# Attention on one core: the new keys' value product in three fp32r passes over split parts, and each reciprocal of a row sum taken one step later

## The reference, cut to what matters

```python
kc = k_cache[block_table].reshape(bsz, L, HK, D)
vc = v_cache[block_table].reshape(bsz, L, HK, D)
k_all = jnp.concatenate([kc, k], axis=1)
v_all = jnp.concatenate([vc, v], axis=1)
...
scores = jnp.einsum('bqhd,bkhd->bhqk', q, k_all) * SCALE
scores = jnp.where(valid[:, None, None, :], scores, -1e+30)
probs = jax.nn.softmax(scores, axis=-1)
o = jnp.einsum('bhqk,bkhd->bqhd', probs, v_all)
```

## Time and profile before

| | |
|---|---|
| median of three runs | 1268.01 us (1266.29 to 1268.69) |
| profiled execution, its own time | 1267.51 us |
| its span, first to last instruction | 1265.5 us |
| busy over the span: PE, PEld, DVE, ACT, POOL | 1232.9, 1036.5, 804.2, 789.2, 749.0 us |
| mean granted TensorE clock | 0.995 |
| attention of the first half, of the second | about 165 to 480 us, 800 to 1112 us |

### The profile page before, as it was taken

How to read it: one execution, slowest core, us unless ns; L and a number is a source line. 1 busy time by engine, 2 the same in 40 slices (tenths; PEclk the granted TensorE clock), 3 DMA queues, 4 the chain that set the end, 5 groups by cost and what they waited for, 6 DMA issues and landing times.

```text
span 1265.5 us, 28738 instructions
## 1 busy us (share of the span) xinstructions
PE 1232.9 (97%) x7378; PEld 1036.5 (82%) x7378; DVE 804.2 (64%) x1725; ACT 789.2 (62%) x2258; POOL 749.0 (59%) x884
## 2 busy tenths in 40 slices
PE   7899999999999999999998999999999999999998
PEld 6678889999999987866776888898999999888756
DVE  5976667667766776952329766676676677655422
ACT  5676677777777774432336666777787777744320
POOL 4344468888888874433233444588888888754330
PEclk9999999999999999999999999999999999999999
DMA  6343289999999955306144342889989999534300
GB/s 236 117 134 124 96 231 231 225 234 232 236 237 235 232 146 183 143 1 200 50 145 125 118 136 101 226 225 233 232 231 238 234 233 237 133 111 152 90 31 34
DMA packets 147979, 214.82 MB, mean 170 GB/s; under 512 B 24950, under 2 KB 119480, under 8 KB 142137
## 3 DMA queue, kind: packets, MB, share of 16 engines
q1 hardware_dynamic: 130568, 204.86, 59.7%
q10 hardware_dynamic: 17328, 9.04, 2.5%
HBM read 203.33 MB, written 10.49 MB: 169 GB/s over the span
## 4 chain that ended last, share of the span: by engine, by line
PE 84%; SPq 5%; DVE 3%; issue 3%; ACT 3%; DMA 1%; ACTq 1%; DVEq 0%
PE PS L1130 16%; PE PS L1098 8%; PE PS L1197 5%; PE PS L992 5%; PE PS L990 5%; PE PS L996 5%; PE PS L1188 5%; PE PS L1194 5%; PE PS L1140 4%; PE PS L976 2%; PE PS L1239 2%; PE PS L1063 2%; SPq L464 2%; PE PS L1065 2%; PE PS L1081 2%
## 5 line engine op out<-in xcount | busy, mean ns | idle before, releaser
L624 POOL TENSOR_TENSOR kv_parts<-kv,k_hi 128x544 fp32r<-128x544 f32 x192 | 258.0, 1344 | 55.0 <-ACT k_hi L806 54.9
L1130 PE MATMUL PS<-probT,kv 128*128 128x128 f32 x2048 | 271.9, 276 | 0.0
L584 POOL TENSOR_TENSOR ring_parts<-ring,kv_parts 128x512 fp32r<-128x512 f32 x96 | 126.2, 1320 | 217.4 <-ACT kv_parts L687 189.2
L1130 PEld LDWEIGHTS PS<-probT,kv 128*128 128x128 f32 x2048 | 250.5, 193 | 0.0
L847 ACT ACTIVATE ring<-ring,smin 128x544 f32<-128x544 f32 x192 | 143.0, 745 | 93.2 <-DVE smin L1618 92.8
L1624 DVE COPY probT<-PS 128x512 f32<-128x512 f32 x256 | 175.5, 685 | 5.4 <-PE PS L1098 5.4
L1618 DVE CUSTOM_DVE_ANT_0 ring<-PS,mask,rq 128x544 f32<-128x544 f32 x192 | 149.8, 780 | 41.5 <-PE PS L1086 31.9
L646 POOL TENSOR_TENSOR ring_parts<-ring,kv_parts 128x512 fp32r<-128x512 f32 x64 | 84.1, 1317 | 100.6 <-ACT kv_parts L897 100.6
L612 POOL TENSOR_SCALAR ring<-ring,rinv 128x512 f32<-128x512 f32 x192 | 133.0, 693 | 0.0
L806 ACT ACTIVATE k_hi<-kv 128x544 fp32r<-128x544 f32 x192 | 124.5, 650 | 8.5 <-DMA kv<-k_new 2.8
L1098 PE MATMUL PS<-consts,ring 128*128 128x128 f32 x768 | 116.6, 275 | 2.1 <-DVE probT L1624 1.7
(11 more groups left out here) (219 smaller groups left out, 2790.4 us busy)
## 6 DMA issues: line engine op xcount, KB each, us to landing
kv<-in_kpages SPq DMA_DIRECT2D x512, 128.0 KB, 2.6
kv<-in_vpages SPq DMA_DIRECT2D x512, 128.0 KB
ring<-in_w SPq DMA_DIRECT2D x44, 1024.0 KB, 5.0
v_new<-kv ACTq DMA_DIRECT2D x16, 256.0 KB, 4.6
k_new<-kv ACTq DMA_DIRECT2D x16, 256.0 KB, 2.4
kv<-k_new SPq DMA_DIRECT2D x32, 128.0 KB, 2.6
kv<-v_new SPq DMA_DIRECT2D x32, 128.0 KB
kv<-in_xT SPq DMA_DIRECT2D x8, 256.0 KB, 5.1
```

The costliest lines, as they stand in the source:

```text
L624: nc.gpsimd.tensor_tensor(kbuf_lo(par)[:, :, g, :], kbuf(par)[:, :, g, :], k_hi[:, e % 2, :].rearrange("p (j t) -> p j t", t=PSIZE), ALU.s ...
L1130: mm = nc.tensor.matmul(PS[:, at:at + D], vbuf(bpar)[:, c, gg * D:(gg + 1) * D], probT[:, g % 2, c * P:(c + 1) * P], start=(c == 0 and a = ...
```

## The change

- `spread` becomes `spread_hi` and `spread_lo`, both fp32r, and the new values get `vnew_hi` (its own place) and `vnew_lo` (in place of the fp32 values). `values_new` issues three fp32r matmuls of 128 by 512 instead of one fp32 matmul.
- ScalarE's `spread_new` writes `spread_hi`, rounded in the copy; VectorE's new `lower_spread` at g = 3 and 7 subtracts it from PSUM, four instructions of 32 by 128. `turn_new`, which writes that PSUM place again, waits for `spread_low`.
- ScalarE's new `upper_values` at g = 5 copies the new values, 128 by 256, rounded; GpSimd's new `lower_values` at the end of step 7 subtracts.
- VectorE takes the reciprocal of step g - 1 in step g, behind the mask and ahead of the copy of bank 4.
- One more memset of 128 by 512 in each half.

```diff
-        spread = kv[:, 2 * (KSZ + VSZ):2 * (KSZ + VSZ) + GU * P]
+        SP_HI, SP_LO, VN_HI = 2 * (KSZ + VSZ), 18944, 19456
+        spread_hi = kv_parts[:, SP_HI:SP_HI + GU * P]
+        spread_lo = kv_parts[:, SP_LO:SP_LO + GU * P]
...
+                def lower_values(b, par):
+
+                    pool.wait_ge(vhi_ready, h * HB + b + 1)
+                    pool.sem_inc(pool_past, 1)
+                    nc.gpsimd.tensor_tensor(vnew_lo(par), vnew(par), vnew_hi(par), ALU.subtract).then_inc(vlo_ready, 1)
+
...
                         elif not first:
                             scale_probs(b - 1, g - 2 + HK)
+                        if g == HK - 1:
+                            lower_values(b, par)
...
+                    nc.scalar.activation(vnew_hi(par), vnew(par), ACT.Copy).then_inc(vhi_ready, 1)
...
-                        pe.wait_ge(spread_ready, GU * (h * QUADS + b * UNITS + u))
+                        pe.wait_ge(spread_low, GU * (h * QUADS + b * UNITS + u))
                     nc.tensor.transpose(PS[:, 2560:2688], prob_new[:, u, :], ident).then_inc(new_turned, 1)
...
-                        pe.wait_ge(spread_clear, h + 1)
-                        pe.wait_ge(first_vnew_in, 16 * (h + 1))
+                        pe.wait_ge(spread_clear, 2 * h + 2)
+                    if u == 0:
+                        pe.wait_ge(vlo_ready, h * HB + b + 1)
                     pe.wait_ge(spread_ready, GU * (h * QUADS + b * UNITS + u + 1))
-                    nc.tensor.matmul(bank(6 + u), vnew(par)[:, u * D:(u + 1) * D], spread, start=False, stop=True)\
-                        .then_inc(o_done, 1)
+                    hi, lo = vnew_hi(par)[:, u * D:(u + 1) * D], vnew_lo(par)[:, u * D:(u + 1) * D]
+                    nc.tensor.matmul(bank(6 + u), hi, spread_hi, start=False, stop=False)
+                    nc.tensor.matmul(bank(6 + u), lo, spread_hi, start=False, stop=False)
+                    pe.wait_ge(spread_low, GU * (h * QUADS + b * UNITS + u + 1))
+                    nc.tensor.matmul(bank(6 + u), hi, spread_lo, start=False, stop=True).then_inc(o_done, 1)
...
+                def lower_spread(b, u):
+
+                    dve.wait_ge(spread_ready, GU * (h * QUADS + b * UNITS + u + 1))
...
+                    for a in range(GU):
+                        rows = slice(a * SEQ, (a + 1) * SEQ)
+                        V.tensor_tensor(spread_lo[rows, a * P:(a + 1) * P], PS[rows, 2560:2688],
+                                        spread_hi[rows, a * P:(a + 1) * P], ALU.subtract).then_inc(spread_low, 1)
...
+                    if g <= HK and not (first and g == 0):
+
+                        k = (g - 1) % HK
+                        dve.wait_ge(exp_done, s)
+                        V.reciprocal(rinv[:, k:k + 1], rsum[:, k:k + 1]).then_inc(rinv_ready, 1)
                     if not (first and g < 3):
...
-                        dve.wait_ge(exp_done, s + 1)
-                        V.reciprocal(rinv[:, g:g + 1], rsum[:, g:g + 1]).then_inc(rinv_ready, 1)
...
+                    if g < HK and g % GU == 3 and not (first and g < GU):
+                        lower_spread(b if g > GU else b - 1, int(g < GU))
```

More of the change, by code:

```diff
@@ L125, in build @@
         KSZ, VSZ = (NPP + 1) * HK * PSIZE, 4 * HK * D + UNITS * D
-        KVSZ = 18944
+        KVSZ = 19968
         with nc.sbuf_tensor("qo_parts", [P, HB * HQ * SEQ], F32R) as qo_parts, \
@@ L200, in vnew, with vnew_hi, vnew_lo @@
             return kv[:, at:at + UNITS * D]
-        spread = kv[:, 2 * (KSZ + VSZ):2 * (KSZ + VSZ) + GU * P]
+        SP_HI, SP_LO, VN_HI = 2 * (KSZ + VSZ), 18944, 19456
+        spread_hi = kv_parts[:, SP_HI:SP_HI + GU * P]
+        spread_lo = kv_parts[:, SP_LO:SP_LO + GU * P]
+        def vnew_hi(u):
+            return kv_parts[:, VN_HI + u * UNITS * D:VN_HI + (u + 1) * UNITS * D]
+        def vnew_lo(u):
+            at = 2 * KSZ + u * VSZ + 4 * HK * D
+            return kv_parts[:, at:at + UNITS * D]
         junk = [prob0[:, 0:512], probT[:, :, :].rearrange("p a x -> p (a x)")[:, 512:1024]]
@@ L355, in build @@
         spread_ready = sem("spread_ready")
+        spread_low = sem("spread_low")
+        vhi_ready = sem("vhi_ready")
+        vlo_ready = sem("vlo_ready")
         o_done = sem("o_done")
@@ L818, in spread_new @@
                     if isinstance(b, int) and b == 0 and u == 0:
-                        act.wait_ge(spread_clear, h + 1)
+                        act.wait_ge(spread_clear, 2 * h + 2)
                     else:
@@ L824, in spread_new, with upper_values @@
                         rows = slice(a * SEQ, (a + 1) * SEQ)
-                        nc.scalar.activation(spread[rows, a * P:(a + 1) * P], PS[rows, 2560:2688], ACT.Copy)\
+                        nc.scalar.activation(spread_hi[rows, a * P:(a + 1) * P], PS[rows, 2560:2688], ACT.Copy)\
                             .then_inc(spread_ready, 1)
+                def upper_values(b, par):
+                    if isinstance(b, int) and b == 0:
+                        act.wait_ge(first_vnew_in, 16 * (h + 1))
+                    else:
+                        n_in = 16 * (NPP + 1)
+                        less = 16 if par == 0 else 0
+                        act.wait_ge(v_in[par], h * (n_in * HB // 2 - less) + (b - par) * (n_in // 2) + n_in - less)
+                    act.sem_inc(act_past, 1)
+                    nc.scalar.activation(vnew_hi(par), vnew(par), ACT.Copy).then_inc(vhi_ready, 1)
                 def keep_o(b, u):
@@ L858, in step @@
                         mask_of(b + 1, 1 - par)
+                    if g == 5:
+                        upper_values(b, par)
                 act.wait_ge(turn_read, h * NQK + NQK - LAG)
@@ L1603, in _ @@
                 norm_rows()
+                def lower_spread(b, u):
+                    dve.wait_ge(spread_ready, GU * (h * QUADS + b * UNITS + u + 1))
+                    if isinstance(b, int) and b == 0 and u == 0:
+                        dve.wait_ge(spread_clear, 2 * h + 2)
+                    dve.sem_inc(dve_past, 1)
+                    for a in range(GU):
+                        rows = slice(a * SEQ, (a + 1) * SEQ)
+                        V.tensor_tensor(spread_lo[rows, a * P:(a + 1) * P], PS[rows, 2560:2688],
+                                        spread_hi[rows, a * P:(a + 1) * P], ALU.subtract).then_inc(spread_low, 1)
                 def step(b, par, g, first):
@@ L1624, in step @@
                         V.tensor_copy(probT[:, (g - 3) % 2, :], bank(4)).then_inc(pt_main, 1)
[L1625 to L1628, removed]
-                        dve.wait_ge(exp_done, s + 1)
-                        V.reciprocal(rinv[:, g:g + 1], rsum[:, g:g + 1]).then_inc(rinv_ready, 1)
[L1632 to L1636, removed]
+                    if g < HK and g % GU == 1:
+                        nb, u = (b, 1) if g == 1 else ((b + 1) % HB, 0)
+                        dve.wait_ge(qhi_ready, h * (QUADS + 1) + b * UNITS + g // GU + 2)
+                        dve.sem_inc(dve_past, 1)
+                        lower_q(u, ds(nb * (HQ * SEQ) + u * GU * D, NS * D))
+                    if g < HK and g % GU == 3 and not (first and g < GU):
+                        lower_spread(b if g > GU else b - 1, int(g < GU))
                 for g in range(HK):
@@ L1642, in _ @@
                         dve.sem_inc(dve_past, 1)
-                        V.memset(spread, 0.0).then_inc(spread_clear, 1)
+                        V.memset(spread_hi.bitcast(F32), 0.0).then_inc(spread_clear, 1)
+                        V.memset(spread_lo.bitcast(F32), 0.0).then_inc(spread_clear, 1)
                 for g in range(HK):
@@ L1652, in _ @@
                 step(HB - 1, 1, HK + 2, False)
+                lower_spread(HB - 1, 1)
                 def lower(head):
```

## The result

| | before | after |
|---|---|---|
| median of the runs, us | 1268.27 (7 runs, 1266.29 to 1272.11) | 1272.25 (7 runs, 1271.46 to 1274.82) |
| span of the profiled execution | 1265.5 | 1273.0 |
| from batch to batch, undisturbed | 19.11 and 19.20 in turn | 19.33 |
| granted clock | 0.995 | 0.995 |

The ratio is 1.0034, 95% interval 1.0022 to 1.0045: 4 us slower, where 13 were forecast. The profiled execution of after took 1274.82, the slowest of its seven, so its span overstates the difference. "Undisturbed" leaves out a few batches in which the kernel waits for loads (19.77 in before; 19.98 and 19.97 in after).

The account below looks back on a forecast made before the run. TensorE was taken as the bound in attention, GpSimd next. A batch: 18.64 + 0.84 + 0.10 = 19.58 against 19.12; 30 x 0.46 = 13.8, less 0.6, gives +13.2 on 1267.5, median 1281 us; range 1262 to 1305.

Parts of the forecast that it names:

- TensorE without waits: TensorE's own work in a batch: 18.96 becomes 18.64, as three fp32r matmuls replace each fp32 call of `values_new`.
- wait for the next batch's key: At the end of a batch TensorE waits for GpSimd's low part of the next key 0: 0.84 a batch.
- wait for the key of step 6: TensorE waiting for the key used in step 6; the prediction listed no such wait, so 0.
- VectorE's copy late: The reciprocal between mask and copy makes three steps of a batch 0.03 late each: 0.10, bounds 0 and 0.4.
- last batches of the two halves, together: The last batch of each half has no passage to a next batch and saves 0.32: -0.6 in all.
- the chain's length: Mask of step 6, reciprocal, GpSimd's two scalings, values' subtraction, next batch's key: from 315.66 to 319.85.
- the spare: Before the change, GpSimd finished the next batch's key 0.78 us earlier than TensorE needed it.
- the cover: In steps 0 and 4 `lower_spread` makes the mask 0.7 late; the copy has 0.8 of room, so nothing is lost.
- The move of the reciprocal alone: Putting the reciprocal of group 5 behind the mask of step 6 delays its end by 1.13, against 0.78 available.
- two engines that block each other: Rival, chance 0.22: VectorE's `lower_q` waits for GpSimd's wide scaling; 0.85 more a batch, 1306 us.
- The faster case: Rival, chance 0.24: GpSimd's chain is off the path, the passage between batches under 0.38 late; -6.6, 1261 us.
- its floor: In the rival where the kernel gets faster, SP's issue of key and value loads becomes the bound: 18.80 a batch.

Follow-up runs that it names:

- e6: The changed kernel without its third pass of the new keys' product (high part of the values by low part of the probabilities): 1265.90 us, ratio 0.9986.
- e4: The kernel before with only the reciprocal moved one step later, values and spread as before: 1264.03 us, ratio 0.9961.
- e2: The changed kernel with GpSimd's subtraction of the values ahead of the scaling of group 5 and ScalarE's copy in step 4: 1261.57 us, ratio 0.9937.

## Why the prediction was right or wrong

The side and the mechanism were right, the size was wrong: +13 forecast, +4 measured, with 1272 inside the range. Term by term, for a batch:

| term | forecast | measured |
|---|---|---|
| TensorE without waits | 18.64 | 2 x 9.32 = 18.64 |
| wait for the next batch's key | 0.84 | 0.63 |
| wait for the key of step 6 | 0 | 0.05 to 0.08 |
| VectorE's copy late | 0.10 | 0 |
| period after | 19.58 | 19.33 |
| period before | 19.12 | 19.15 |
| last batches of the two halves, together | -0.6 | -0.9 |
| bare `lower_spread` behind the second half | 0 | +0.6 |

The difference is 0.18 a batch instead of 0.46; 30 x 0.18 = 5.4, with the two last rows 5.1. The last matmul starts 6.1 later (1260.91 and 1267.05); 0.6 of the rest is one batch of 19.98 in the first half of after, in which TensorE waits for value pages. Behind the last matmul's start the profiled executions differ by another 1.4 (4.6 of 1265.5, and 6.0 of 1273.0), where the change touches nothing. The medians lie 4.0 apart, and the 2 us between 6.1 and 4.0 are within the spread of either kernel's runs.

The step that failed is the size of the wait for the next batch's key: forecast 0.84, measured 0.63. The forecast of a batch is 0.28 too dear: 0.21 for this wait, 0.10 for the copy, 0.03 for a before that was taken 0.03 too short, less the 0.05 to 0.08 of the key of step 6, which was put at nothing. Piece by piece:

- *The wait, 0.84 for 0.63.* The subtraction takes 0.69 to the next instruction's start, not 0.79; the two scalings 0.91, not 0.95; the mask of step 6 starts 0.38 behind the transposes, as a mask that waits does, not 0.42. That is 0.18 of the 0.21, in a chain of 4.6. The prediction had the difference of two large numbers, the chain's length less the spare, and an error of 4% in the chain is a fifth of the wait. The reciprocal's end (0.87 behind the mask's start) and GpSimd's start (0.20 behind it) were right to the hundredth.
- *The copy, 0.10 for 0.* The reciprocal was priced as 0.16 and a gap of 0.06. In the rows the copy starts 0.07 behind the reciprocal's start, 0.78 behind the mask's instead of 0.93: in these rows each of the two starts before the one ahead of it has ended.
- *`lower_spread`*, 1.23 for 1.2, the mask 0.56 late for 0.7, and nothing lost at the copy: right. But the cover was thinner than the prediction said. It followed the mask to the copy only; by way of the reciprocal and GpSimd the mask also sets the key of step 6, and there the room was used up in after (0.05 to 0.08 is lost at that key), and e6 fell into it.
- *The ends of the halves* were priced as a gain. The last batches do gain, 0.44 each (18.95 and 4.83 to 18.57 and 4.77), but the last `lower_spread` lies bare behind the second.
- *The move of the reciprocal alone* "is more than the whole spare": e4 shows that it isn't. The 0.37 by which the narrow scaling gets shorter was in the sum but not in that sentence.

Of the rivals: two engines that block each other did so, but the one held up was GpSimd, at a place with idle time behind it. The Trainium skill, SBUF — State Buffer, "Who interferes with whom", has the later of the two wait to the end; here they overlapped and GpSimd's took 0.37 longer, so a wait of VectorE for GpSimd's whole instruction isn't seen. The prediction took the earlier trace rows for a case in which VectorE came first; by those rows GpSimd's narrow scaling started first too (315.64, `lower_q` 315.65), and paid 0.37 there as well. The faster case needed a passage less than 0.38 late and got one 0.63 late; moving the subtraction (e2) brings it about, and then its floor (18.8 a batch, 1261) held to within 1 us. That the loads bound e2 shows in the first third of each half: three batches take SP 19.6 to 20.7 each there, and three of the kernel take 19.2 to 19.8, and from the first `values_new` of a half to the last e2 gains 3.0 and 3.7, not 15 times the 0.37 that an undisturbed batch gains; the fast case had 3.0 a half. In its even batches 18.78 is as much the key of steps 2 and 6 as the loads' 18.77, and no run parts the two in e2.

## What to carry to other kernels

What an added instruction costs is set by its place: 0.73 of GpSimd cost 0.63 behind the scaling that waits for the reciprocal, and nothing ahead of it, in the idle time of that same wait, once what it waits for itself had been moved up too. Follow a late instruction by every way on which something reads it, since the room on one (the copy) says nothing of the room on another (the key of step 6). Time each of two edits with and without the other: the reciprocal's move was worth 5 us alone and 35 beside the passes.

## What was not expected of the hardware

- A reciprocal of one column, 0.16 by its row, delays the next instruction on VectorE by 0.07 when neither waits; the 256-column subtraction on GpSimd takes 0.73 and delays the next by 0.69.
- GpSimd's scaling of 512 columns took 1.06 instead of 0.69 where VectorE's two-input subtraction of 384 columns started 0.01 after it (mean of 64: 1026 ns, in before 696); VectorE's took 0.57 as elsewhere.
- A third score matmul that has to wait for its weights costs 0.11 beyond the wait, since the fourth follows 0.24 behind it instead of 0.13.
